# Relational graph layer on one core: x's high part by a rounding copy with a test of its low bits, VectorE's small steps with two inputs, and a new order in the head

## The chip, the cores and the metric

The kernel runs on one NeuronCore of a Trainium2 chip. The metric is the device time of one execution, in microseconds (us). A core has TensorE (PE) for matrix products, VectorE (DVE), ScalarE (ACT) and GpSimd (POOL) for elementwise work, and SyncE (SP), which here issues the large transfers. Each works through its own list in order and waits on semaphores for the others.

## What is computed

x is 8 x 1024 x 128 (fp32), adj is 8 x 1024 x 1024 (int32, here only 0 and 1), weight 4 x 128 x 128, bias 128. Per batch and relation the nodes' features are summed over the edges of that relation and projected, the input is added, and each row is normalised:

```python
masks = (relation[None] == rel_ids[:, None, None, None]).astype(x.dtype)
h = jnp.einsum('rbnm,bmd->rbnd', masks, x)
y = jnp.einsum('rbnd,rdo->bno', h, weight)
out = layernorm(x + y + bias)          # (v - mean) / sqrt(var + 1e-5) over the 128 features
```

With the inputs as drawn only relation 1 occurs. The kernel computes that case and counts on the way whether another value occurs; if one did, a general path behind a branch would be run (not entered here).

## The kernel before, in words

**Units and halves.** adj comes in 32 units of 1 MB (4 per batch, 256 target nodes each), x in 8 loads of 0.5 MB. Two units make a half (512 nodes), so there are 16 halves, called hf 0 to 15 below. SP issues the loads in the order unit 0, x of batch 0, unit 1, and so on; unit u waits until unit u - 8 has been masked (8 buffers), and x of batch b from batch 4 on until batch b - 4 has been added (4 buffers). The stores stand behind all loads in SP's list.

**Per unit.** VectorE turns the integers into bytes (`convert`, L429: min with 2, times 60, u32 to u8, 128 x 2048). TensorE transposes them as packed words (`turn`, L178). ScalarE expands the bytes into fp32r numbers (`expand`, L350).

**Per half.** TensorE multiplies the expanded mask by x in two parts, 8 matmuls of 512 columns each: `hi_products` with x_hi and `lo_products` with x_lo (L187). ScalarE copies the sum out of PSUM (`copy_half`, L357), TensorE spreads the bias (L194) and multiplies by the weights (L199, together `project_half`), VectorE adds x (`add_half`, L443) and takes statistics (L205, L210) and var + eps (`lift_variance`, L214), GpSimd raises that to the power -0.5 and makes the scale and shift of each row (`scales`: L307, L217, L312), and VectorE (`normalize`, L221) and ScalarE (L370) write two row groups each. The first and the last half go in quarters (256 nodes).

**The two parts of x, per batch.** VectorE masks x down to its upper 20 bits (`top`, L166, x_top), GpSimd copies x_top into x_hi as fp32r (`hi`, L297) and subtracts it from x (`lo`, L170, x_lo).

**The order.** All lists are written by hand. TensorE in the loop, for half hf: hi_products(hf), turn(2hf + 3), project_half(hf - 1), lo_products(hf), turn(2hf + 4). VectorE in the loop, for hf: convert(2hf + 4), convert(2hf + 5), on even hf top of the batch after the current one, add_half(hf - 1) with its statistics and var + eps, and normalize of half hf - 2. GpSimd: hi(b + 1), scales(2b - 1), lo(b + 1), scales(2b). In the head VectorE runs convert(0), top(0), `place_bias` (three copies of the bias's bf16 parts, L491), convert(1) to convert(3), top(1), convert(4) and on. Dummy matmuls (`keep_warm`, L605) fill TensorE's first waits.

## Time and profile before

| | before |
|---|---|
| runs | 119.49 us median of 3 (118.33 to 120.13) |
| the profiled execution | 118.53 us, span 116.7 us, mean granted TensorE clock 0.991 |
| busy | PE 102.6 us (88%), DVE 95.0 (81%), ACT 84.6 (72%), POOL 75.7 (65%) |
| loads and stores | 42.16 MB; HBM read 37.82 MB; mean 361 GB/s over the span |

The span is what the profile covers; the execution's own time lies 1.83 us above it. "Busy" leaves out waits, branches and the issuing of transfers. The whole-span shares mix a head (up to about 28 us), a steady stretch (28 to 104 us) and a tail. In the page's 40 slices the DMA engines are at nine tenths or more from the second slice to the 33rd, and TensorE from about the tenth.

### The profile page before, as it was taken

How to read it: one execution, taken by the hardware profiler on the slowest of the kernel's cores; microseconds unless marked ns; L12 is line 12 of the kernel's file. 1: busy time of each engine (PE TensorE's matmuls, PEld its weight loads, DVE VectorE, ACT ScalarE, POOL GpSimd, SP SyncE). 2: the span in 40 equal slices, each digit the busy share in tenths (PEclk: the TensorE clock that was granted, in tenths of full speed). 3: DMA queues.
4: the chain of work that ended last, by engine and by line, in shares of the span. 5: the costliest groups of instructions: out<-in, count | busy, mean ns of one | idle time of the engine just before them, and what ended most of it. 6: DMA issues, size and time to landing. Idle time of an engine off the chain costs nothing.

```text
span 116.7 us, 1943 instructions
## 1 busy us (share of the span) xinstructions
PE 102.6 (88%) x587; PEld 85.5 (73%) x587; DVE 95.0 (81%) x242; ACT 84.6 (72%) x114; POOL 75.7 (65%) x78
## 2 busy tenths in 40 slices
PE   5966379994999999999999999999999999999800
PEld 2333378683889888888898889898888888889600
DVE  0089967633989899999999999999999999996960
ACT  0433199179868997899999999999999889974410
POOL 6069038000095998599759898999899759953640
PEclk9999999999999999999999999999999999999996
DMA  3999999999999999999999999999999997030441
GB/s 87 396 433 429 415 438 427 415 432 418 418 424 424 424 424 417 417 424 424 414 431 421 414 428 413 429 413 427 421 427 418 404 420 314 10 142 38 171 152 53
DMA packets 7362, 42.16 MB, mean 361 GB/s; under 512 B 819, under 2 KB 1206, under 8 KB 3254
## 3 DMA queue, kind: packets, MB, share of 16 engines
q1 hardware_dynamic: 7200, 41.95, 86.9%
q8 instruction: 6, 0.10, 0.4%
q10 hardware_dynamic: 150, 0.07, 0.2%
q14 instruction: 6, 0.05, 0.1%
HBM read 37.82 MB, written 4.19 MB: 360 GB/s over the span
## 4 chain that ended last, share of the span: by engine, by line
PE 48%; DMA 21%; DVE 15%; POOL 8%; issue 3%; ACTq 1%; POOLq 0%; DVEq 0%
PE h_ps L187 32%; DMA adj_sb<-in_adj_dram 17%; PE y_ps L199 8%; PE tp_ps L178 7%; DMA bias_rows<-in_L_gnn_bias_dram 4%; DVE bias_parts L491 4%; POOL scale L217 4%; DVE mask L429 3%; DVE stats L205 3%; POOL x_lo L170 2%; DVE total L443 2%; PE y_ps L194 2%; DVE var_eps L214 2%; DVE mean_var L210 1%; ACTq L379 1%
## 5 line engine op out<-in xcount | busy, mean ns | idle before, releaser
L350 ACT ACTIVATE maskT<-tp_ps 128x2048 fp32r<-128x2048 fp8e5 x32 | 60.2, 1881 | 14.9 <-PE tp_ps L178 14.8
L429 DVE TENSOR_SCALAR mask<-adj_sb 128x2048 uint8<-128x2048 uint32 x32 | 39.5, 1267 | 12.4 <-DMA adj_sb<-in_adj_dram 12.4
L217 POOL TENSOR_TENSOR scale<-var_eps,power 128x4 f32<-128x4 f32 (+1 forms) x17 | 36.3, 2137 | 0.9 <-DVE var_eps L214 0.7
L187 PE MATMUL h_ps<-maskT,x_hi 128*128 128x512 f32 (+1 forms) x144 | 34.2, 379 | 2.6 <-ACT maskT L350 2.5
L187 PE MATMUL h_ps<-maskT,x_lo 128*128 128x512 f32 (+1 forms) x144 | 34.3, 380 | 0.4 <-POOL x_lo L170 0.4
L187 PEld LDWEIGHTS h_ps<-maskT,x_hi 128*128 128x128 f32 x144 | 24.3, 189 | 7.7 <-ACT maskT L350 3.9
L187 PEld LDWEIGHTS h_ps<-maskT,x_lo 128*128 128x128 f32 x144 | 24.1, 189 | 4.5 <-POOL x_lo L170 0.7
L178 PEld LDWEIGHTS tp_ps<-identity,mask 128*128 128x128 f32 x128 | 19.8, 202 | 6.4 <-DVE mask L429 2.7
L178 PE MATMUL tp_ps<-identity,mask 128*128 128x128 f32 x128 | 20.2, 281 | 3.4 <-DVE mask L429 3.4
L170 POOL TENSOR_TENSOR x_lo<-x_sb,x_top 128x1024 fp32r<-128x1024 f32 x8 | 19.2, 2402 | 0.0
L307 POOL TENSOR_SCALAR minus_mean<-mean_var 128x4 f32<-128x4 f32 (+1 forms) x16 | 4.0, 248 | 22.5 <-DVE var_eps L214 21.6
L199 PEld LDWEIGHTS y_ps<-w_sb,h_sb 128*128 128x128 f32 x128 | 16.7, 192 | 1.2 <-ACT h_sb L364 0.7
L199 PE MATMUL y_ps<-w_sb,h_sb 128*128 128x128 f32 x128 | 17.2, 276 | 0.3 <-ACT h_sb L364 0.3
L205 DVE BATCH_NORM_STATS2 stats<-total 128x6 f32<-128x128 f32 x64 | 14.1, 281 | 1.3
L370 ACT ACTIVATE out_sb<-total,shift,scale 128x128 f32<-128x128 f32 x31 | 13.5, 484 | 0.8 <-POOL shift L312 0.6
L297 POOL CAST x_hi<-x_top 128x1024 fp32r<-128x1024 f32 x8 | 8.3, 1041 | 6.9 <-DVE x_top L166 6.9
L357 ACT ACTIVATE h_sb<-h_ps 128x512 f32<-128x512 f32 x14 | 8.4, 599 | 5.5 <-issue 5.5
L443 DVE TENSOR_TENSOR total<-y_ps,x_sb 128x512 f32<-128x512 f32 (+1 forms) x17 | 11.0, 650 | 0.8 <-PE y_ps L199 0.8
L221 DVE TENSOR_SCALAR out_sb<-total,mean_var,scale 128x128 f32<-128x128 f32 x33 | 9.9, 339 | 0.6 <-POOL scale L217 0.6
L214 DVE TENSOR_SCALAR var_eps<-mean_var 128x4 f32<-128x4 f32 (+1 forms) x17 | 8.3, 485 | 1.7
L605 PE MATMUL h_ps<-warm 128*128 128x512 bf16 x24 | 7.6, 478 | 1.4 <-POOL warm L275 1.4
L312 POOL TENSOR_TENSOR shift<-minus_mean,scale 128x4 f32<-128x4 f32 (+1 forms) x16 | 6.0, 372 | 2.1
(30 smaller groups left out, 40.4 us busy)
## 6 DMA issues: line engine op xcount, KB each, us to landing
adj_sb<-in_adj_dram SPq DMA_DIRECT2D x32, 1024.0 KB, 18.0
x_sb<-in_x_dram SPq DMA_DIRECT2D x8, 512.0 KB, 12.1
out_dram<-out_sb SPq DMA_DIRECT2D x7, 512.0 KB, 18.5
out_dram<-out_sb SPq DMA_DIRECT2D x1, 256.0 KB, 2.3
out_dram<-out_sb SPq DMA_DIRECT2D x2, 128.0 KB, 2.6
w_sb<-in_L_gnn_weight_dram ACTq DMA_DIRECT2D x1, 64.0 KB, 7.1
bias_rows<-in_L_gnn_bias_dram ACTq DMA_DIRECT2D x3, 0.5 KB
```

The costliest lines, as they stand in the source:

```text
L170: eng.tensor_tensor(flat(x_lo[:, slot]), flat(x_sb[:, x_slot]), flat(x_top[:, :]).bitcast(fp32), ALU.subtract).then_inc(done, 1)
L178: last = nc.tensor.transpose(tp_ps[:, bank, place:place + P], words[:, o, j], identity[:, :])
L187: last = nc.tensor.matmul(h_ps[:, bank, 0:n], (x_hi, x_lo)[part][:, slot, t, :], maskT[:, places, t // WORD, t % WORD, :], start=(first an ...
L199: last = nc.tensor.matmul(y[:, n, :], h_of(r)[:, s], w_sb[:, r, :], start=False, stop=(r == relations - 1 and s == tiles.stop - 1))
L205: last = nc.vector.bn_stats(stats[:, slot, s, :], total[:, place, s, :])
L214: nc.vector.tensor_scalar(var_eps[:, slot, tiles], mean_var[:, slot, tiles, 1], EPS, None, ALU.add).then_inc(done, by)
L217: nc.gpsimd.tensor_tensor(scale[:, slot, tiles], var_eps[:, slot, tiles], power[:, tiles], ALU.pow).then_inc(done, by)
L221: last = nc.vector.tensor_scalar(out_sb[:, b, s, :], total[:, place, s, :], mean_var[:, slot, s, 0:1], scale[:, slot, s:s + 1], ALU.subtra ...
L350: nc.scalar.activation(maskT[:, u % NMT], turned_codes(u % NTP), ACT.Copy, accum_out=counts[:, u:u + 1]).then_inc(expanded, 1)
L370: last = nc.scalar.activation(out_sb[:, b, s, :], total[:, b % NTOTAL, s, :], ACT.Identity, bias=shift[:, b % 2, s:s + 1], scale=scale[:, ...
L429: nc.vector.tensor_scalar(mask[:, u % NMASK], adj_sb[:, u % NADJ].bitcast(u32), CAP, SET, ALU.min, ALU.mult).then_inc(masked, 1)
L443: nc.vector.tensor_tensor(total[:, b % NTOTAL, tiles], y, x_sb[:, b % NX, tiles], ALU.add).then_inc(added, by)
```

## The change

- **x's high part.** VectorE's mask of x and its buffer x_top go. x_hi is now a copy of x into fp32r, which rounds; x_lo is x minus x_hi. For batch 0 VectorE makes both itself, from batch 1 on GpSimd does.
- **The test.** Before its first var + eps (half 0) VectorE takes the low 12 bits of both slots of x_hi, finds their maximum and adds it to eps. If the copies left any low bit set, eps would become huge; otherwise it stays 1e-5.
- **Small steps.** `lift_variance` adds a tile eps in place of a constant; `normalize` takes the scale as a second tensor, broadcast over the row.
- **GpSimd's order.** lo follows hi at once, both ahead of the scales of the iteration, and lo(b) waits until unit 4b + 1 has been masked.
- **The head.** The bias copies are a quarter as wide and stand behind convert(2), since the matmul now broadcasts the bias itself. project_half(1) moves from behind turn(7) to behind turn(5), with ScalarE's copy_half(1) between expand(4) and expand(5).

VectorE's list from the add of half 0 to the next two masks, before (L429 is convert; the first row is convert(7), the rows after the stats belong to half 0, the last two rows are convert(8) and convert(9)):

```order
L429 TENSOR_SCALAR mask<-adj_sb 128x2048 [waits turned,adj_loaded7]
L443 TENSOR_TENSOR total<-y_ps,x_sb 128x512 [waits projected]
L205 BN_STATS stats<-total 128x6 [waits added]
L205 BN_STATS stats<-total 128x6 x3
L210 BN_AGGR mean_var<-stats 128x2 [waits measured]
L210 BN_AGGR mean_var<-stats 128x2 x3
L214 TENSOR_SCALAR var_eps<-mean_var 128x4 [waits aggregated]
L429 TENSOR_SCALAR mask<-adj_sb 128x2048 [waits turned,adj_loaded0]
L429 TENSOR_SCALAR mask<-adj_sb 128x2048 [waits turned,adj_loaded1]
```

The same place in the changed kernel (L433 is convert there, L450 the add):

```order
L433 TENSOR_SCALAR mask<-adj_sb 128x2048 [waits turned,adj_loaded7]
L450 TENSOR_TENSOR total<-y_ps,x_sb 128x512 [waits projected]
L204 BN_STATS stats<-total 128x6 [waits added]
L204 BN_STATS stats<-total 128x6 x3
L438 TENSOR_SCALAR low_bits<-x_hi 128x2048 [waits hi_made,const_set]
L441 TENSOR_REDUCE low_most<-low_bits 128x1 [waits low_found]
L443 TENSOR_TENSOR eps<-eps,low_most 128x8 [waits low_found]
L209 BN_AGGR mean_var<-stats 128x2 [waits measured,low_found]
L209 BN_AGGR mean_var<-stats 128x2 x3
L214 TENSOR_TENSOR var_eps<-mean_var,eps 128x4 [waits aggregated]
L433 TENSOR_SCALAR mask<-adj_sb 128x2048 [waits turned,adj_loaded0]
L433 TENSOR_SCALAR mask<-adj_sb 128x2048 [waits turned,adj_loaded1]
```

Three instructions, two of them over 2048 elements per partition, stand ahead of the masks of units 8 and 9.

GpSimd's list from the second scales on, before (x_hi and x_lo of batches 2 and 3; L307, L217 and L312 are one call of `scales`):

```order
L297 CAST x_hi<-x_top 128x1024 [waits multiplied,topped]
L307 TENSOR_SCALAR minus_mean<-mean_var 128x4 [waits var_ready]
L217 TENSOR_TENSOR scale<-var_eps,power 128x4
L312 TENSOR_TENSOR shift<-minus_mean,scale 128x4 [waits negated,scaled]
L170 TENSOR_TENSOR x_lo<-x_sb,x_top 128x1024
L307 TENSOR_SCALAR minus_mean<-mean_var 128x4 [waits var_ready]
L217 TENSOR_TENSOR scale<-var_eps,power 128x4
L312 TENSOR_TENSOR shift<-minus_mean,scale 128x4 [waits negated,scaled]
L297 CAST x_hi<-x_top 128x1024 [waits multiplied,topped]
```

And in the changed kernel:

```order
L300 CAST x_hi<-x_sb 128x1024 [waits multiplied,x_loaded2]
L168 TENSOR_TENSOR x_lo<-x_sb,x_hi 128x1024 [waits masked,hi_made]
L312 TENSOR_SCALAR minus_mean<-mean_var 128x4 [waits var_ready]
L217 TENSOR_TENSOR scale<-var_eps,power 128x4
L317 TENSOR_TENSOR shift<-minus_mean,scale 128x4 [waits negated,scaled]
L312 TENSOR_SCALAR minus_mean<-mean_var 128x4 [waits var_ready]
L217 TENSOR_TENSOR scale<-var_eps,power 128x4
L317 TENSOR_TENSOR shift<-minus_mean,scale 128x4 [waits negated,scaled]
L300 CAST x_hi<-x_sb 128x1024 [waits multiplied,x_loaded3]
```

The subtraction has moved from between the two scales to directly behind the copy.

The diff, without the tile and semaphore declarations, the general path and the renamed sites:

```diff
...
@@ -162,12 +164,8 @@
         def store(eng, b, place, tiles, done):
             eng.dma_start(out_p[b][:, tiles.start * D:tiles.stop * D], flat(out_sb[:, place, tiles])).then_inc(done, 16)
 
-        def take_top(x_slot, done):
-            nc.vector.tensor_scalar(flat(x_top[:, :]), flat(x_sb[:, x_slot]).bitcast(u32), TOP_BITS, None,
-                                    ALU.bitwise_and).then_inc(done, 1)
-
         def take_lo(eng, x_slot, slot, done):
-            eng.tensor_tensor(flat(x_lo[:, slot]), flat(x_sb[:, x_slot]), flat(x_top[:, :]).bitcast(fp32),
+            eng.tensor_tensor(flat(x_lo[:, slot]), flat(x_sb[:, x_slot]), flat(x_hi[:, slot]).bitcast(fp32),
                               ALU.subtract).then_inc(done, 1)
 
         def turn_words(of, bank, done):
@@ -191,7 +189,8 @@
 
         def spread_bias(y, tiles):
             n = tiles.stop - tiles.start
-            nc.tensor.matmul(y[:, 0:n, :], spread[:, :], bias_parts[:, 0:n, :], start=True, stop=False)
+            nc.tensor.matmul(y[:, 0:n, :], spread[:, :], bias_parts[:, :].unsqueeze(1).to_broadcast([P, n, D]),
+                             start=True, stop=False)
 
         def project(h_of, y, relations, tiles, done, by):
             for n, s in enumerate(range(tiles.start, tiles.stop)):
@@ -211,15 +210,16 @@
             last.then_inc(done, by)
 
         def lift_variance(slot, tiles, done, by):
-            nc.vector.tensor_scalar(var_eps[:, slot, tiles], mean_var[:, slot, tiles, 1], EPS, None, ALU.add).then_inc(done, by)
+            n = tiles.stop - tiles.start
+            nc.vector.tensor_tensor(var_eps[:, slot, tiles], mean_var[:, slot, tiles, 1], eps[:, 0:n], ALU.add).then_inc(done, by)
 
         def row_scales(slot, tiles, done, by):
             nc.gpsimd.tensor_tensor(scale[:, slot, tiles], var_eps[:, slot, tiles], power[:, tiles], ALU.pow).then_inc(done, by)
 
         def normalize(b, slot, place, tiles, done, by):
             for s in tiles:
-                last = nc.vector.tensor_scalar(out_sb[:, b, s, :], total[:, place, s, :], mean_var[:, slot, s, 0:1],
-                                               scale[:, slot, s:s + 1], ALU.subtract, ALU.mult)
+                last = nc.vector.scalar_tensor_tensor(out_sb[:, b, s, :], total[:, place, s, :], mean_var[:, slot, s, 0:1],
+                                                      scale[:, slot, s:s + 1].to_broadcast([P, D]), ALU.subtract, ALU.mult)
             last.then_inc(done, by)
 
         block = ctx.enter_context(nc.Block())
@@ -279,8 +279,9 @@
             nc.gpsimd.affine_select(identity[:, :], ones[:, :], [[-1, P]], ALU.is_equal, 0.0, base=0,
                                     channel_multiplier=1).then_inc(const_set, 1)
             nc.gpsimd.memset(power[:, :], -0.5).then_inc(const_set, 1)
+            nc.gpsimd.memset(eps[:, :], EPS).then_inc(const_set, 1)
             nc.gpsimd.memset(spread[:, :], 1.0).then_inc(const_set, 1)
-            nc.gpsimd.memset(bias_parts[:, :, :], 0.0).then_inc(bias_split, 1)
+            nc.gpsimd.memset(bias_parts[:, :], 0.0).then_inc(bias_split, 1)
 
             def split_bias():
                 pool.wait_ge(bias_loaded, 16 * len(PARTS))
@@ -291,12 +292,16 @@
                                         ALU.subtract).then_inc(bias_split, 1)
 
             def hi(b):
-                pool.wait_ge(topped, b + 1)
-                if b >= 2:
+                pool.wait_ge(x_loaded[b % NX], 16 * (b // NX + 1))
+                if b == 1:
+                    pool.wait_ge(lo_made, 1)
+                else:
                     pool.wait_ge(multiplied, CH * (b - 1))
-                nc.gpsimd.tensor_copy(flat(x_hi[:, b % 2]), flat(x_top[:, :]).bitcast(fp32)).then_inc(hi_made, 1)
+                nc.gpsimd.tensor_copy(flat(x_hi[:, b % 2]), flat(x_sb[:, b % NX])).then_inc(hi_made, 1)
 
             def lo(b):
+                pool.wait_ge(hi_made, b + 1)
+                pool.wait_ge(masked, CH * b + 2)
                 take_lo(nc.gpsimd, b % NX, b % 2, lo_made)
 
             def scales(b, tiles, count, by):
@@ -316,15 +321,12 @@
                 scales(hf // 2, HALF[hf % 2], 2 * (hf + 1), 2)
 
             split_bias()
-            hi(0)
-            lo(0)
             for b in range(B):
                 if b + 1 < B:
                     hi(b + 1)
+                    lo(b + 1)
                 if b >= 1:
                     scales_half(2 * b - 1)
-                if b + 1 < B:
-                    lo(b + 1)
                 scales_half(2 * b)
             scales(LAST, QUARTER[2], 2 * (HALVES - 1) + 1, 1)
             pool.wait_ge(var_ready, 2 * HALVES)
...
@@ -384,8 +385,11 @@
             expand(2)
             copy_quarter(0, 1)
             expand(3)
-            for hf in range(1, HALVES - 1):
-                if hf >= 2:
+            expand(4)
+            copy_half(1)
+            expand(5)
+            for hf in range(2, HALVES - 1):
+                if hf > 2:
                     copy_half(hf - 1)
                 expand(2 * hf + 2)
                 expand(2 * hf + 3)
@@ -429,12 +433,15 @@
                 nc.vector.tensor_scalar(mask[:, u % NMASK], adj_sb[:, u % NADJ].bitcast(u32), CAP, SET,
                                         ALU.min, ALU.mult).then_inc(masked, 1)
 
-            def top(b):
-                dve.wait_ge(x_loaded[b % NX], 16 * (b // NX + 1))
-                if b >= 1:
-                    dve.wait_ge(hi_made, b)
-                    dve.wait_ge(lo_made, b)
-                take_top(b % NX, topped)
+            def find_low_bits():
+                dve.wait_ge(hi_made, 2)
+                nc.vector.tensor_scalar(low_bits[:, :], x_hi[:, :].rearrange("p s t d -> p (s t d)").bitcast(u32), ~TOP_BITS & 0xFFFFFFFF, None,
+                                        ALU.bitwise_and).then_inc(low_found, 1)
+                dve.wait_ge(low_found, 1)
+                nc.vector.reduce_max(low_most[:, :], low_bits[:, :], AX.X).then_inc(low_found, 1)
+                dve.wait_ge(low_found, 2)
+                nc.vector.tensor_tensor(eps[:, :], eps[:, :], low_most[:, :].to_broadcast([P, TILES]), ALU.add).then_inc(low_found, 1)
+                dve.wait_ge(low_found, 3)
 
             def add(b, y, tiles, count, by):
                 dve.wait_ge(projected, count)
@@ -447,6 +454,10 @@
                 measure_rows(b % 2, b % NTOTAL, tiles, measured, by)
 
             def variances(b, tiles, count, by):
+                if count == 2:
+                    dve.wait_ge(const_set, 5)
+                if count == 2:
+                    find_low_bits()
                 dve.wait_ge(measured, count)
                 aggregate_rows(b % 2, tiles, aggregated, by)
                 dve.wait_ge(aggregated, count)
@@ -488,24 +499,24 @@
             def place_bias():
                 dve.wait_ge(bias_split, 3)
                 for q, part in zip(PARTS, (bias_rows, bias_rest, bias_fine)):
-                    last = nc.vector.tensor_copy(bias_parts[q:q + 1], upper(part[q:q + 1, :]).unsqueeze(1).to_broadcast(
-                        [1, HT, D]))
+                    last = nc.vector.tensor_copy(bias_parts[q:q + 1, :], upper(part[q:q + 1, :]))
                 last.then_inc(bias_split, 1)
 
             convert(0)
-            top(0)
+            dve.wait_ge(x_loaded[0], 16)
+            nc.vector.tensor_copy(flat(x_hi[:, 0]), flat(x_sb[:, 0])).then_inc(hi_made, 1)
+            dve.wait_ge(hi_made, 1)
+            take_lo(nc.vector, 0, 0, lo_made)
+            convert(1)
+            convert(2)
             place_bias()
-            for u in (1, 2, 3):
-                convert(u)
-            top(1)
+            convert(3)
             convert(4)
             convert(5)
             for hf in range(1, HALVES - 1):
                 for u in (2 * hf + 4, 2 * hf + 5):
                     if u < UNITS:
                         convert(u)
-                if hf % 2 == 0 and hf // 2 + 1 < B:
-                    top(hf // 2 + 1)
                 add_half(hf - 1)
                 measure_half(hf - 1)
                 if hf >= 2:
...
@@ -624,12 +635,14 @@
             turn(4)
             lo_products(1)
             turn(5)
+            project_half(1)
             turn(6)
             for hf in range(2, HALVES - 1):
                 hi_products(hf)
                 if 2 * hf + 3 < UNITS:
                     turn(2 * hf + 3)
-                project_half(hf - 1)
+                if hf > 2:
+                    project_half(hf - 1)
                 lo_products(hf)
                 if 2 * hf + 4 < UNITS:
                     turn(2 * hf + 4)
...
```

The declarations add `low_bits` (128 x 2048, u32), `low_most` (128 x 1) and `eps` (128 x 8), drop `x_top`, and make `bias_parts` 128 x 128.

## Rows read from the trace of the kernel before

**Rows 1.** The page: busy tenths, granted clock and GB/s moved in 40 slices of the span.
```profile
PE   5966379994999999999999999999999999999800
PEclk9999999999999999999999999999999999999996
GB/s 87 396 433 429 415 438 427 415 432 418 418 424 424 424 424 417 417 424 424 414 431 421 414 428 413 429 413 427 421 427 418 404 420 314 10 142 38 171 152 53
```

**Rows 2.** TensorE in order of time: start us, us, engine, line, what, [idle before <- releaser].
```profile
13.50 0.75 PE L178 MATMUL tp_ps<-identity,mask 128*128 128x128 f32 x4 [2.50 <-DVE mask L429]
...
33.43 0.63 PE L178 MATMUL tp_ps<-identity,mask 128*128 128x128 f32 x4
37.26 2.10 PE L187 MATMUL h_ps<-maskT,x_lo 128*128 128x512 f32 x8
39.20 0.63 PE L178 MATMUL tp_ps<-identity,mask 128*128 128x128 f32 x4
43.46 2.14 PE L187 MATMUL h_ps<-maskT,x_lo 128*128 128x512 f32 x8 [0.20 <-POOL x_lo L170]
...
101.68 2.13 PE L187 MATMUL h_ps<-maskT,x_lo 128*128 128x512 f32 x8 [0.17 <-POOL x_lo L170]
```

**Rows 3.** VectorE in order of time, from convert(7) to convert(8).
```profile
28.30 1.23 DVE L429 TENSOR_SCALAR mask<-adj_sb 128x2048 uint8<-128x2048 uint32 x1 [3.86 <-DMA adj_sb<-in_adj_dram]
29.44 0.68 DVE L443 TENSOR_TENSOR total<-y_ps,x_sb 128x512 f32<-128x512 f32 x1
30.16 0.87 DVE L205 BATCH_NORM_STATS2 stats<-total 128x6 f32<-128x128 f32 x4
31.07 0.38 DVE L210 BATCH_NORM_AGGREGATE mean_var<-stats 128x2 f32<-128x6 f32 x4
31.55 0.17 DVE L214 TENSOR_SCALAR var_eps<-mean_var 128x4 f32<-128x4 f32 x1
31.66 1.23 DVE L429 TENSOR_SCALAR mask<-adj_sb 128x2048 uint8<-128x2048 uint32 x1
```

**Rows 4.** Groups by line and form: count | busy us, mean ns | idle before them.
```profile
L443 DVE TENSOR_TENSOR total<-y_ps,x_sb 128x512 f32<-128x512 f32 x15 | 10.2, 681 | 0.8 <-PE y_ps L199 0.8
L443 DVE TENSOR_TENSOR total<-y_ps,x_sb 128x256 f32<-128x256 f32 x2 | 0.8, 414 | 0.0
```

**Rows 5.** VectorE in order of time, an undisturbed pass of the steady loop.
```profile
81.02 0.68 DVE L443 TENSOR_TENSOR total<-y_ps,x_sb 128x512 f32<-128x512 f32 x1
...
83.19 0.17 DVE L214 TENSOR_SCALAR var_eps<-mean_var 128x4 f32<-128x4 f32 x1
...
83.78 2.36 DVE L429 TENSOR_SCALAR mask<-adj_sb 128x2048 uint8<-128x2048 uint32 x2
86.05 0.68 DVE L443 TENSOR_TENSOR total<-y_ps,x_sb 128x512 f32<-128x512 f32 x1
```

**Rows 6.** GpSimd in order of time: a copy, two ends of scales, a subtraction.
```profile
46.88 1.05 POOL L297 CAST x_hi<-x_top 128x1024 fp32r<-128x1024 f32 x1 [0.61 <-DVE x_top L166]
51.98 0.20 POOL L312 TENSOR_TENSOR shift<-minus_mean,scale 128x4 f32<-128x4 f32 x1
...
75.15 0.20 POOL L312 TENSOR_TENSOR shift<-minus_mean,scale 128x4 f32<-128x4 f32 x1
75.30 2.39 POOL L170 TENSOR_TENSOR x_lo<-x_sb,x_top 128x1024 fp32r<-128x1024 f32 x1
```

**Rows 7.** VectorE in order of time, beside the scales and the subtraction.
```profile
49.43 2.38 DVE L429 TENSOR_SCALAR mask<-adj_sb 128x2048 uint8<-128x2048 uint32 x2
...
71.79 2.35 DVE L429 TENSOR_SCALAR mask<-adj_sb 128x2048 uint8<-128x2048 uint32 x2
76.25 1.47 DVE L214 TENSOR_SCALAR var_eps<-mean_var 128x4 f32<-128x4 f32 x1
```

**Rows 8.** The warm-up matmuls in order of time, the first two batches of them.
```profile
1.38 4.72 PE L605 MATMUL h_ps<-warm 128*128 128x512 bf16 x12 [1.38 <-POOL warm L275]
7.57 1.89 PE L605 MATMUL h_ps<-warm 128*128 128x512 bf16 x8
```

19 lines of the change are left out of this document (10 added, 9 removed).

## The prediction, made before the changed kernel was run

> **What bounds the kernel now.** I read the page first: TensorE's row of tenths stands at nine from the tenth slice on, with the granted clock at nine almost throughout, and the transfers move some 420 GB/s up to the 33rd [rows 1]. Then TensorE in order of time [rows 2]. From the start of the loop near 28 us it runs back to back: turn(8) starts at 33.43, turn(10) at 39.20, so one half takes **5.77 us**. From lo_products(3) at 37.26 to lo_products(14) at 101.68 there are 11 halves, 64.42 us, against 11 x 5.77 = 63.47: only 0.95 us is lost in all that time, and where the rows name a cause it is x_lo, late from GpSimd (43.46, 101.68). Whatever delays TensorE in this stretch delays the end by as much, since nothing behind it has slack to give back; whatever is saved there can be at most 0.95 us. The question is therefore when TensorE gets into its stride, and whether VectorE keeps ahead of it.
>
> VectorE's head [rows 3]: convert(1) to convert(3) stand behind the bias copies, and TensorE waits 2.50 us for the first of them [rows 2]. But convert(7) starts at 28.30 after 3.86 us of waiting for the transfer of unit 7. From there VectorE works in order: add at 29.44, statistics at 30.16, mean and variance at 31.07, var + eps at 31.55, convert(8) at 31.66.
>
> **The head.** Bias copies that are a quarter as wide and stand behind convert(2) let units 1 to 3 be masked as they arrive. VectorE takes on the copy and the subtraction of batch 0, about 0.7 us (1024 columns at a convert's pace) and 1.2 us (by the 1.04 ns per column worked out below), between convert(0) and convert(1), while unit 1 is still being loaded. With project_half(1) moved ahead, TensorE should be through hi_products(2) before unit 7 is masked. None of it moves the landing of unit 7, which was issued before anything that changes here. So convert(7) stays at 28.30 and is ready at 29.53; turn(7), project_half(1) being done already, and lo_products(2) (1.94 us to the next turn, 37.26 to 39.20 [rows 2]) let TensorE stand ready for turn(8) near 31.9 instead of 33.43. I book the head's repair at **0**: what it gains is waited away at the next point. The cover is the transfer of unit 7; were that earlier, the gain would show (see the rivals).
>
> **The test of low bits.** Three instructions stand on VectorE between the statistics of half 0 and convert(8). The masking of 128x2048 u32 has the input of a convert: 1.23 us [rows 3]. The maximum over 2048 columns has no row. The adds give (681 - 414) / 256 = 1.04 ns per column and 0.15 us fixed [rows 4], so 2048 columns make 2.28 us; the lower bound is a convert's 1.23, the upper the statistics' pace, 512 columns in 0.87 us, so 3.5 us [rows 3]. I take 2.28: one pass at the add's pace. The small add is 0.17, as var + eps, and three waits on its own results take 0.05 each. Sum 1.23 + 2.28 + 0.17 + 0.15 = 3.83 us, between 2.8 and 5.0. Then mean and variance start at 31.07 + 3.83 = 34.90, convert(8) 0.59 later at 35.49, its mask is ready at 36.72, and turn(8) starts near 36.78 instead of 33.43: **+3.35 us**, between +2.3 and +4.6. It is not hidden: TensorE's list is in order, turn(8) stands ahead of hi_products(3), and TensorE waits for it some 4.9 us.
>
> **x's parts, without x_top.** Eight masks of x leave VectorE, and x_lo is made an iteration and more before lo_products wants it. The 0.95 us of the steady stretch goes: **-0.95**. VectorE's pass without a mask of x is 86.05 - 81.02 = 5.03 us [rows 5], well under 5.77.
>
> But GpSimd now holds VectorE at another place. The trace shows that the two exclude each other: var + eps, normally 0.17 us, took 1.47 at 76.25, until the x_lo of 75.30 + 2.39 had ended, and VectorE's next converts with it [rows 6, 7]. In the changed list the scales of the odd pass are followed by hi and lo in one go. Two calls show when the scales end: their last step started 0.17 us after the end of the two converts beside it in one (51.98 against 49.43 + 2.38), 1.01 us after in the other (75.15 against 71.79 + 2.35) [rows 6, 7]. The copy starts 0.15 us after that and takes 1.05, the subtraction 0.05 later 2.39: it ends 3.81 to 4.65 us after the converts. The next convert would start 5.03 - 2.36 = 2.67 us after them [rows 5] and is held 1.14 to 1.98 us.
>
> The first such place is convert(10). With convert(8) at 35.49 the pair ends at 37.85, the subtraction of batch 2 at 41.66 to 42.50, and mask 10 is ready at 42.9 to 43.7; TensorE wants it at 36.78 + 5.77 = 42.55. That costs 0.35 to 1.2 us, **+0.8**. Later, two passes take 10.06 + (1.14 to 1.98) = 11.2 to 12.0 us against TensorE's 11.54: 0 to 0.5 us in each of five pairs. The middle is 0.1 over: **+0.4**, between 0 and 2.5.
>
> **Small steps and tail.** var + eps and normalize change their form. var + eps and two normalizes took 0.59 us of a pass (83.19 to 83.78) [rows 5]; two normalizes at 128 x 1.04 ns + 0.15 us alone would be 0.57. Booked at 0, since they stand where VectorE is ahead; what they could cost at most is the first rival below. The narrower bias copies and the broadcast bias matmul: 0; they stand in waits of the head.
>
> **Sum.** +3.35 - 0.95 + 0.8 + 0.4 = +3.6 us. On the profiled execution's 118.53 that makes 122.1; that execution is 0.96 under the median of the runs, from which it would be 123.1. I forecast **122.6 us**, between the two. With the bounds (+2.3 - 0.95 + 0.35 to +4.6 - 0.95 + 1.2 + 2.5) this case covers 120.2 to 126.8, and I hold 121.0 to 124.9 for its likely part.
>
> **Rivals.**
>
> *VectorE becomes the bound, because the new small steps are held too.* The rows leave open whether a step with two inputs from SBUF waits for GpSimd: the only such form before is the add, whose first input is PSUM, and its 15 instances average 0.681 us, hence never waited long [rows 4]. If they wait, the var + eps and two normalizes, 0.59 us by the rows of a pass, come behind the subtraction rather than ahead of it: a pair takes 11.8 to 12.6, 0.3 to 1.1 us over TensorE's, 0.7 x 5 = 3.5 in place of 0.4, and the first place costs 0.6 more. Together +3.7: about 126. It decides once a pair exceeds 11.54 us. For it speaks that both inputs must be read at once; against it that VectorE then gains what it waits less elsewhere. The Trainium skill, "SBUF — State Buffer", section "Who interferes with whom", says that a VectorE instruction with two SBUF inputs contends with a GpSimd instruction that reads SBUF, which speaks for this rival and against what the change does to the small steps; no row here shows such an instruction. Chance 0.15.
>
> *TensorE's clock falls in the 4.9 us wait for turn(8).* The granted clock of the trace stays at full until the tail [rows 1]; its longest wait is 2.50 us, and the 13.50 row behind it is quick [rows 2]. But the first 12 warm-up matmuls took 4.72 us, 393 ns each, the later eight 236 ns [rows 8]: after idleness it ran at the pace of its lower level for about 4 us and lost some 2. If that comes again: about 124.6. The Trainium skill, "TensorE: Matmul & The Clock Gate", section "What's actually happening", has the clock halved after idleness; this trace has no wait long enough to tell. Chance 0.15.
>
> *Not slower: unit 7 lands earlier.* Its wait of 3.86 us is long against the 2.5 us that a megabyte takes at the page's some 420 GB/s [rows 1, 3]. Were it masked 2.3 us earlier, at 26.0, turn(8) would start at 34.4, +1.0 us; with -0.95 and the collisions at their lower bound of 0.35 the sum is +0.4, 119 to 120. From 3.35 us earlier on the test costs nothing. For it speaks that units before it came evenly; against it that the order of issue up to unit 8 is the same. Halfway, at 26.9, it gives 121 to 121.5. Chance 0.25, a fifth of it faster by over 2%, where VectorE's freed time also does more than I can see.
>
> **Chances and range.** 2% of 119.49 is 2.4 us, about what a measurement of this kernel can tell from no change. The forecast case has 0.45, of which a tenth of all chances lies below 121.9. Slower by over 2%: 0.35 + 0.15 + 0.15 = 0.65, and with a little of the last rival 0.67. Within 2%: 0.28. Faster: 0.05. The range that should hold 8 in 10 is 120.2 to 126.0.
>
> **What would show it.** In the new profile: a wait of TensorE of 4 to 5 us for mask 8 between about 32 and 37 us; a reduce of low_bits near 2.3 us; convert(8) near 35.5; then 5.77 us per half with no wait for x_lo; single waits for masks where the subtraction stands beside a convert that took up to 3 us; matmuls of 8 in 2.1 us right after the long wait, if the clock held. I am wrong if convert(8) starts before 33, if unit 7's mask is well before 28.3, or if TensorE keeps losing time for masks through the whole loop.

## The result, and the profile after

The changed kernel takes **122.99 us** (median of 4 runs, 122.8 to 123.46) against 119.81 us for the kernel before beside it (4 runs, 118.33 to 120.8): a ratio of **1.035** [1.025, 1.045], slower. Its profiled execution took 122.80 us, span 121.1, mean granted clock 0.977. Ratios, here and below, compare of either kernel only the runs within 1.5% of its fastest, so they differ somewhat from the ratios of the medians. The time lies 0.4 us from the 122.6 forecast; the sum behind it is right in its main term and wrong in two others, which nearly cancelled.

The page of the kernel after, as in [rows 1]: busy tenths, granted clock and GB/s in 40 slices.

```profile
PE   5988799976609999999999999999999999999800
PEclk9999999999995899999999999999999999999996
GB/s 89 403 430 429 424 424 425 411 425 428 420 425 422 425 406 430 425 417 421 429 414 422 421 429 420 409 430 425 420 422 413 402 260 0 0 41 133 156 158 54
```

TensorE has a hole in slices 11 and 12 (6, 0), and right behind it the granted clock falls for two slices (5, 8). Neither is in the rows of before.

VectorE in order of time, answering to [rows 3]:

```profile
28.29 1.23 DVE L433 TENSOR_SCALAR mask<-adj_sb 128x2048 uint8<-128x2048 uint32 x1 [2.34 <-DMA adj_sb<-in_adj_dram]
...
30.94 1.21 DVE L438 TENSOR_SCALAR low_bits<-x_hi 128x2048 uint32<-128x2048 uint32 x1
32.19 2.29 DVE L441 TENSOR_REDUCE low_most<-low_bits 128x1 f32<-128x2048 uint32 x1
34.51 0.17 DVE L443 TENSOR_TENSOR eps<-eps,low_most 128x8 f32<-128x8 f32 x1
...
35.30 2.36 DVE L433 TENSOR_SCALAR mask<-adj_sb 128x2048 uint8<-128x2048 uint32 x2
...
39.79 2.72 DVE L221 SCALAR_TENSOR_TENSOR out_sb<-total,mean_var,scale 128x128 f32<-128x128 f32 x2
42.43 2.35 DVE L433 TENSOR_SCALAR mask<-adj_sb 128x2048 uint8<-128x2048 uint32 x2
```

convert(7) still starts when unit 7 lands. Behind it stand the mask of the low bits, the reduce of 2.29 us and the small add; convert(8) starts at 35.30, 3.64 us later than before. Further down two normalizes took 2.72 us, held by the x_lo that GpSimd was making (it ended at 42.36); convert(10) waited for them, and mask 10 was ready at 43.6, within the 42.9 to 43.7 of the prediction.

TensorE in order of time, answering to [rows 2]:

```profile
36.58 1.00 PE L176 MATMUL tp_ps<-identity,mask 128*128 128x128 f32 x4 [4.38 <-DVE mask L433]
37.23 3.52 PE L185 MATMUL h_ps<-maskT,x_hi 128*128 128x512 f32 x8
40.58 0.63 PE L176 MATMUL tp_ps<-identity,mask 128*128 128x128 f32 x4
...
44.04 0.63 PE L176 MATMUL tp_ps<-identity,mask 128*128 128x128 f32 x4
...
105.87 2.12 PE L185 MATMUL h_ps<-maskT,x_lo 128*128 128x512 f32 x8
```

turn(8) starts 3.15 us later than before, after a wait of 4.38 us. Eight matmuls behind it take 3.52 us instead of some 2.1, and turn(9) starts 4.00 us after turn(8). Before it was 2.34 (33.43 to 35.77): 1.66 us lost to the clock. TensorE then runs without a wait for x_lo to lo_products(14), 4.19 us later than at 101.68. The windows of the same stretch say what the clock was. Each row has the stretch, its length, the busy time of PE, PEld, DVE, ACT and POOL (with the number of instructions), the granted clock, the DMA share and GB/s:

```profile
32.00:36.50 4.50, 0.20 (x1) 0.00 (x0) 4.29 (x10) 0.89 (x3) 0.97 (x1) 1.00 1.02 424
36.50:38.00 1.50, 1.42 (x6) 1.32 (x7) 1.50 (x3) 0.39 (x1) 1.50 (x2) 0.64 0.99 415
38.00:40.60 2.60, 2.60 (x9) 2.00 (x8) 2.43 (x12) 1.58 (x2) 2.39 (x4) 0.55 1.01 422
40.60:46.00 5.40, 5.40 (x33) 4.72 (x32) 5.37 (x7) 4.45 (x6) 4.42 (x4) 1.00 1.01 417
```

0.55 to 0.64 of full speed while TensorE was busy again: mostly the lower level, 1.2 GHz. At 40.6 it was back at 2.4. Through the wait itself it still stood at full; it fell as TensorE resumed.

Two rows of the steady loop show GpSimd beside VectorE, answering to [rows 6, 7]; first GpSimd (scale, shift, x_hi, x_lo), then VectorE:

```profile
47.28 1.39 POOL L217 TENSOR_TENSOR scale<-var_eps,power 128x4 f32<-128x4 f32 x1
48.80 1.02 POOL L317 TENSOR_TENSOR shift<-minus_mean,scale 128x4 f32<-128x4 f32 x1
49.76 1.03 POOL L300 CAST x_hi<-x_sb 128x1024 fp32r<-128x1024 f32 x1
50.87 2.39 POOL L168 TENSOR_TENSOR x_lo<-x_sb,x_hi 128x1024 fp32r<-128x1024 f32 x1
```

```profile
46.88 0.60 DVE L221 SCALAR_TENSOR_TENSOR out_sb<-total,mean_var,scale 128x128 f32<-128x128 f32 x2
47.41 2.35 DVE L433 TENSOR_SCALAR mask<-adj_sb 128x2048 uint8<-128x2048 uint32 x2
...
51.79 1.49 DVE L214 TENSOR_TENSOR var_eps<-mean_var,eps 128x4 f32<-128x4 f32 x1
...
53.73 2.35 DVE L433 TENSOR_SCALAR mask<-adj_sb 128x2048 uint8<-128x2048 uint32 x2
```

var + eps in its two-input form is held, 1.49 us instead of 0.16, until x_lo ends at 53.26. But the power at 47.28 takes only 1.39 us, beside the converts. In the kernel before it mostly ended behind the converts and averaged 2.32 us; three of its instances beside a pair of converts were short there too, this one among them:

```profile
54.87 1.38 POOL L217 TENSOR_TENSOR scale<-var_eps,power 128x4 f32<-128x4 f32 x1
```

In the changed kernel all ten that start during a normalize with converts behind it take 1.39 or 1.40 us. The pair of converts that starts at 53.73 has its like two passes later at 65.10, so two passes take 11.37 us, under TensorE's 11.60: the loop loses nothing.

### The profile page after: what moved, and what is told of

Read it like the earlier page. It is cut to its first block, busy times and chain, and to the rows that moved or that the text cites. A ratio compares the mean times of both kernels' runs of the same rounds, so it can differ in the third digit from the quotient of the medians.

```text
span 121.1 us, 1941 instructions
## 1 busy us (share of the span) xinstructions
PE 105.0 (87%) x586; PEld 86.4 (71%) x587; DVE 93.8 (77%) x239; ACT 84.8 (70%) x114; POOL 64.3 (53%) x77
## 3 DMA queue, kind: packets, MB, share of 16 engines
HBM read 37.82 MB, written 4.19 MB: 347 GB/s over the span
## 4 chain that ended last, share of the span: by engine, by line
PE 61%; DMA 18%; DVE 9%; SPq 4%; issue 3%; POOL 1%; POOLq 0%; DVEq 0%
PE h_ps L185 39%; DMA adj_sb<-in_adj_dram 18%; PE tp_ps L176 10%; PE y_ps L198 10%; SPq L159 3%; PE y_ps L192 2%; DVE low_most L441 2%; DVE stats L204 2%; DVE total L450 1%; SPq L162 1%; DVE mask L433 1%; DVE low_bits L438 1%; POOL scale L217 1%; DVE mean_var L209 1%; DVE out_sb L221 1%
## 5 line engine op out<-in xcount | busy, mean ns | idle before, releaser
L433 DVE TENSOR_SCALAR mask<-adj_sb 128x2048 uint8<-128x2048 uint32 x32 | 38.0, 1219 | 16.2 <-DMA adj_sb<-in_adj_dram 16.2
L185 PE MATMUL h_ps<-maskT,x_hi 128*128 128x512 f32 (+1 forms) x144 | 35.8, 392 | 0.4 <-ACT maskT L351 0.3
L185 PEld LDWEIGHTS h_ps<-maskT,x_hi 128*128 128x128 f32 x144 | 25.4, 198 | 5.7 <-ACT maskT L351 1.4
L176 PE MATMUL tp_ps<-identity,mask 128*128 128x128 f32 x128 | 21.1, 288 | 7.6 <-DVE mask L433 7.6
L217 POOL TENSOR_TENSOR scale<-var_eps,power 128x4 f32<-128x4 f32 (+1 forms) x17 | 23.1, 1358 | 0.7 <-DVE var_eps L214 0.7
L312 POOL TENSOR_SCALAR minus_mean<-mean_var 128x4 f32<-128x4 f32 (+1 forms) x16 | 4.0, 251 | 31.3 <-DVE var_eps L214 31.3
L168 POOL TENSOR_TENSOR x_lo<-x_sb,x_hi 128x1024 fp32r<-128x1024 f32 x7 | 16.8, 2394 | 5.8 <-DVE mask L433 5.3
L450 DVE TENSOR_TENSOR total<-y_ps,x_sb 128x512 f32<-128x512 f32 (+1 forms) x17 | 11.0, 649 | 2.6 <-issue 1.8
L221 DVE SCALAR_TENSOR_TENSOR out_sb<-total,mean_var,scale 128x128 f32<-128x128 f32 x33 | 12.2, 408 | 0.6 <-POOL scale L217 0.6
L317 POOL TENSOR_TENSOR shift<-minus_mean,scale 128x4 f32<-128x4 f32 (+1 forms) x16 | 11.0, 689 | 2.4 <-POOL scale L217 0.5
L300 POOL CAST x_hi<-x_sb 128x1024 fp32r<-128x1024 f32 x7 | 7.2, 1035 | 6.3 <-DMA x_sb<-in_x_dram 6.3
L214 DVE TENSOR_TENSOR var_eps<-mean_var,eps 128x4 f32<-128x4 f32 (+1 forms) x17 | 9.2, 540 | 1.6
```

Of the source, the lines that this page charges most:

```text
L168: eng.tensor_tensor(flat(x_lo[:, slot]), flat(x_sb[:, x_slot]), flat(x_hi[:, slot]).bitcast(fp32), ALU.subtract).then_inc(done, 1)
L176: last = nc.tensor.transpose(tp_ps[:, bank, place:place + P], words[:, o, j], identity[:, :])
L185: last = nc.tensor.matmul(h_ps[:, bank, 0:n], (x_hi, x_lo)[part][:, slot, t, :], maskT[:, places, t // WORD, t % WORD, :], start=(first an ...
L217: nc.gpsimd.tensor_tensor(scale[:, slot, tiles], var_eps[:, slot, tiles], power[:, tiles], ALU.pow).then_inc(done, by)
L221: last = nc.vector.scalar_tensor_tensor(out_sb[:, b, s, :], total[:, place, s, :], mean_var[:, slot, s, 0:1], scale[:, slot, s:s + 1].to_b ...
L317: nc.gpsimd.tensor_tensor(shift[:, b % 2, tiles], minus_mean[:, b % 2, tiles], scale[:, b % 2, tiles], ALU.mult).then_inc(shifted, by)
```

## The experiments

The eleven kernels came in several sets, each with its own runs of the kernel before. Those runs spread from 117.2 to 121.6 us, so differences well under 1 us between sets rest on the traces, not on the medians.

### 1. Without the test

```diff
-                if count == 2:
-                    find_low_bits()
```

> The changed kernel without the three instructions of the low-bits test (low_bits, low_most and the add to eps); the check on x_hi is left out, the rest is computed. Theory A (the test delays TensorE at turn(8), and the long wait brings its clock down): convert(8) at about 31.7 us, or when its unit lands, turn(8) near 32.9 instead of 36.6, no slow matmuls behind it, the granted clock of the span back near 0.99; x_lo never late; span about 121.1 - 3.7 - 1.7 = 115.7 to 116.2, time about 117.8, 1 to 1.5% under the kernel before. Rival B (the delay comes from GpSimd's new order and the two-input steps): at most 1 us less than the changed kernel, about 122.

Measured 118.8 us (118.32 to 119.14), ratio 1.002 [0.998, 1.006]. So **the test costs 4.2 us** of the changed kernel's time (122.99 against 118.8), all of the change's loss. The kernel comes out 1 us above the 117.8 expected, and TensorE in order of time says where:

```profile
33.10 0.75 PE L176 MATMUL tp_ps<-identity,mask 128*128 128x128 f32 x4 [0.81 <-DVE mask L433]
...
40.13 0.74 PE L176 MATMUL tp_ps<-identity,mask 128*128 128x128 f32 x4 [0.95 <-DVE mask L433]
```

turn(10) waits 0.95 us, since var + eps is held there by batch 2's x_lo. VectorE of the same kernel:

```profile
36.61 1.81 DVE L214 TENSOR_TENSOR var_eps<-mean_var,eps 128x4 f32<-128x4 f32 x1
```

That is the collision at mask 10 of the prediction (+0.8). In the full change nothing shows of it, since TensorE, slowed by its clock, came later than the mask.

### 2. The test in the head's waits

```diff
+            take_low_bits()                # behind convert(5)
...
+                    if u == 6:
+                        find_low_most()    # reduce and add, ahead of convert(7)
...
-                    find_low_bits()
+                    dve.wait_ge(low_found, 3)
```

> The changed kernel with the same test cut in two and moved into VectorE's two waits for transfers in the head: the masking of the low bits behind convert(5), the maximum and the add to eps behind convert(6). Theory A: the waits of 2.7 and 2.3 us (before convert(6) and convert(7)) hold 1.2 and 2.5 us of work, so convert(7) is at most 0.3 us late, the x_lo of batch 1 starts about 1 us later without being late for lo_products(2), and the time is that of the kernel without the test within 0.4 us, about 118: the test costs nothing, only its place did. Rival B (the head is too tight: the masking and x_lo exclude each other and hold convert(6) and turn(6)): convert(7) or turn(6) slips by 1 us or more and the time is 119 to 120.

Measured 119.23 us (119.04 to 119.56), 1.007 [1.001, 1.012]: 0.4 us over no test, 3.8 under the change. VectorE:

```profile
21.95 1.22 DVE L438 TENSOR_SCALAR low_bits<-x_hi 128x2048 uint32<-128x2048 uint32 x1
24.62 1.85 DVE L433 TENSOR_SCALAR mask<-adj_sb 128x2048 uint8<-128x2048 uint32 x1 [1.45 <-DMA adj_sb<-in_adj_dram]
26.39 2.27 DVE L443 TENSOR_REDUCE low_most<-low_bits 128x1 f32<-128x2048 uint32 x1
28.78 1.23 DVE L433 TENSOR_SCALAR mask<-adj_sb 128x2048 uint8<-128x2048 uint32 x1
```

The reduce, 2.27 us again, lies in the wait for unit 7; convert(7) is 0.4 late, because convert(6) took 1.85 beside batch 1's x_lo. The test's place is its cost.

### 3. TensorE kept busy in the wait

```diff
                 lo_products(hf)
+                if hf == 2:
+                    for _ in range(18):
+                        nc.tensor.matmul(h_ps[:, 0, :], warm[:, 0:P], warm[:, :], start=True, stop=True)
```

> The changed kernel with 18 dummy matmuls of 512 columns between lo_products(2) and turn(8), about 3.9 us of work in the 4.4 us that TensorE waits there; their product is thrown away. Theory A (1.66 us of the loss is the clock's, turn(8) to turn(9) in 4.00 us against 2.34): turn(8) stays at 36.6, turn(9) follows in 2.34 us, the granted clock returns to about 0.99, span 1.5 to 1.7 us shorter, about 121.3 us. It could be up to 1 us less, since VectorE's mask 10 (ready at 43.7) is then wanted at 42.4. Rival B (the slow matmuls behind the wait have another cause, such as the transfers or the weights): turn(9) still takes 4.0 us, time as the changed kernel or longer.

Measured 122.36 us (122.23 to 122.46), 1.035 [1.032, 1.039]. TensorE:

```profile
31.87 4.06 PE L649 MATMUL h_ps<-warm 128*128 128x512 bf16 x18
36.43 0.75 PE L176 MATMUL tp_ps<-identity,mask 128*128 128x128 f32 x4 [0.49 <-DVE mask L433]
36.93 2.12 PE L185 MATMUL h_ps<-maskT,x_hi 128*128 128x512 f32 x8
38.88 0.63 PE L176 MATMUL tp_ps<-identity,mask 128*128 128x128 f32 x4
...
43.56 0.75 PE L176 MATMUL tp_ps<-identity,mask 128*128 128x128 f32 x4 [1.06 <-DVE mask L433]
```

The clock held: 2.12 us for the eight matmuls, turn(9) 2.45 after turn(8). But of 1.55 us saved only 0.6 reach the end (0.5 by the spans), because now turn(10) waits 1.06 us. The clock's loss and the collision at mask 10 lie over each other; alone the first costs 1.6 us and the second 1.0.

### 4. The test alone, on the kernel before

The test and the tile eps (set by GpSimd, read by var + eps as a scalar), and nothing else of the change; the call:

```diff
             def variances(b, tiles, count, by):
+                if count == 2:
+                    dve.wait_ge(const_set, 5)
+                    find_low_bits()
```

> The kernel before with the test alone, at the same place as in the change (eps as a tile that var + eps reads as a per-row scalar). Theory A (the test is nearly the whole of the loss): convert(8) near 35.4, turn(8) near 36.6, TensorE's wait is 3.1 us here since its head is not repaired; if the clock falls as in the changed kernel +4.8 us, if not +3.2 us, against the kernel before: 122.7 to 124.3 us. Rival B (the test costs no more than VectorE's idle time): under 1 us more, about 120.3.

Measured 122.26 us (121.55 to 123.63), 1.034 [1.024, 1.045], as much as the whole change, but by another way than expected. Unit 7 had landed at 26.91, so convert(8) started at 33.95 and mask 8 was ready at about 35.2; turn(8) started at 35.51 without a wait. In this execution the test delayed no turn. TensorE was 2.08 us late there (33.43 before) through the head:

```profile
14.46 1.13 PE L182 MATMUL tp_ps<-identity,mask 128*128 128x128 f32 x4 [3.20 <-DVE mask L434]
15.24 2.06 PE L191 MATMUL h_ps<-maskT,x_lo 128*128 128x256 f32 x8
...
93.62 2.12 PE L191 MATMUL h_ps<-maskT,x_lo 128*128 128x512 f32 x8 [0.28 <-POOL x_lo L174]
```

Here the 3.20 us wait for mask 1 was enough for the clock to fall: 2.06 us for eight matmuls of 256 columns that take 1.20 in the kernel before, granted clock 0.50 from 14 to 17 us. (The bias's rows arrived later: GpSimd began to split them at 8.07 us, in the kernel before at 6.79, and the bias copies stand ahead of mask 1.) The loop lost 1.9 us more: from lo_products(3) to lo_products(14) it took 66.33 us against 64.42, with six waits for x_lo like the last row, and the power took 3.33 to 3.94 us each of the ten times that it started just ahead of converts. Whether the test brought that about isn't shown. So this kernel doesn't give the test's price; experiments 1 and 2 do. Unit 7's landing, on which my third rival stood, differs by 1.6 us between executions (26.91 to 28.47 over the eleven profiled ones in which the mask waits for it alone).

### 5. The head's repair alone

The edits of `spread_bias`, `place_bias`, project_half(1) and the order of the head, as in the diff of the change; x's parts, small steps and GpSimd's order as before.

> The kernel before with the head's repair alone: narrow bias copies behind convert(2), the bias broadcast by the matmul, project_half(1) and copy_half(1) ahead; x_top, GpSimd's order and the one-input steps as before, no test. Theory C (the head's worth is that TensorE's clock no longer falls in its wait for mask 1; where it held, as in the profiled execution of before, it is worth nothing): mask 1 ready at 12.6 instead of 13.5, held by GpSimd's first x_lo; granted clock of the span 0.985 or more in every run, time 118 to 118.7 with a spread under 1 us, against 117.8 to 121.1 for the kernel before. Rival D (the spread of the kernel before has another cause): spread over 2 us here too. If a half still takes 5.77 us here, the 5.80 of the changed kernel comes from neither the bias's broadcast nor the head.

Measured 118.3 us (12 runs, 117.12 to 120.47) against 119.51 (24 runs), 0.995 [0.990, 1.001]. The wait for mask 1 shrinks from 2.50 to 1.76 us and turn(8) starts at 32.63, 0.8 earlier, with convert(7) at 27.99. Near 0, as booked, and if anything a gain.

Theory C failed in its signs: the runs spread over 3.35 us and not under 1, at granted clocks of 0.971 to 0.994, as rival D had it. The profiled execution is one of the longer ones (119.27 us), though its clock never fell before the tail. What it lost lies in the loop, 65.89 us from lo_products(3) to lo_products(14) against 64.42, mostly where x_lo came late:

```profile
102.46 2.13 PE L187 MATMUL h_ps<-maskT,x_lo 128*128 128x512 f32 x8 [0.17 <-POOL x_lo L170]
```

So the spread of the kernel before has at least one cause beside the clock.

### 6. The small steps with one input

```diff
-            nc.vector.tensor_tensor(var_eps[...], mean_var[...], eps[:, 0:n], ALU.add)
+            nc.vector.tensor_scalar(var_eps[...], mean_var[...], eps[:, 0:1], None, ALU.add)
...
-                last = nc.vector.scalar_tensor_tensor(..., scale[:, slot, s:s + 1].to_broadcast([P, D]), ...)
+                last = nc.vector.tensor_scalar(..., scale[:, slot, s:s + 1], ...)
```

> The changed kernel with var + eps and normalize in their one-input form (eps and the scale as per-row scalars). Theory E (both forms are held by GpSimd's copy and subtraction until these end, so the form changes nothing): var + eps takes up to 1.5 us beside x_lo, the first normalize pair up to 2.7, turn(8) at 36.6 and the clock's fall as in the changed kernel, time 122.5 to 123.3. Rival F (the two-input form is what is held, or what spares GpSimd's power of 1.4 us against 2.1): the DVE rows beside x_lo are short, or the power takes 2 us and more again, and TensorE waits for masks in the loop, 0.5 us or more either way.

Measured **126.12 us** (125.48 to 126.47), 1.065 [1.060, 1.070]: 3.1 us slower than the change, where my theory said no difference. GpSimd and then VectorE, both with one-input steps:

```profile
47.55 3.33 POOL L217 TENSOR_TENSOR scale<-var_eps,power 128x4 f32<-128x4 f32 x1
...
51.16 1.04 POOL L300 CAST x_hi<-x_sb 128x1024 fp32r<-128x1024 f32 x1
52.27 2.49 POOL L168 TENSOR_TENSOR x_lo<-x_sb,x_hi 128x1024 fp32r<-128x1024 f32 x1
...
67.00 1.40 POOL L217 TENSOR_TENSOR scale<-var_eps,power 128x4 f32<-128x4 f32 x1
```

```profile
47.15 0.60 DVE L221 TENSOR_SCALAR out_sb<-total,mean_var,scale 128x128 f32<-128x128 f32 x2
47.66 2.36 DVE L433 TENSOR_SCALAR mask<-adj_sb 128x2048 uint8<-128x2048 uint32 x2
...
52.19 2.66 DVE L221 TENSOR_SCALAR out_sb<-total,mean_var,scale 128x128 f32<-128x128 f32 x2
54.77 1.24 DVE L433 TENSOR_SCALAR mask<-adj_sb 128x2048 uint8<-128x2048 uint32 x1
```

The power starts 0.1 us ahead of the convert as in the change, but ends 0.9 us behind both converts (3.33 us). The scales, x_hi and x_lo all end later, and the converts wait longer: from 54.77 to 67.14, two passes take 12.37 us, over TensorE's 11.6. TensorE then waits for a mask in each pair, five times between 56 and 106 us, four of them 0.46 to 0.48. The power is not long every time: four of the nine that start during a normalize with converts behind it take 1.39 or 1.40 us, as at 67.00. Each of these follows directly on an x_lo that had held the normalizes.

### 7. Which of the two small steps

The change with one of the two steps back in the one-input form: first var + eps, then the normalizes.

> The changed kernel with var + eps in its one-input form again (scalar eps[:, 0:1]) and the normalizes left with two inputs. Theory G: what the two-input form is worth (122.99 against 126.12 us) comes from the normalizes. GpSimd's power starts 0.1 us before the first convert in both kernels (47.28 against 47.41, and 47.55 against 47.66), so it isn't its own start that differs but what VectorE executes just then: a two-input normalize leaves it a way in, a one-input one doesn't. Then this kernel takes 123.0 us (122.6 to 123.4), power 1.4 us each time, two passes 11.4 us. Theory V: var + eps does it, since it stands directly ahead of GpSimd's three steps. Then 126.1 us, power 3.3 us beside free converts. Both in part: 124 to 125.5.

> The changed kernel with the normalizes in their one-input form and var + eps left with two inputs. Theory G: 126.1 us (125.7 to 126.5), power 3.3 us beside free converts, two passes near 12.4 us or, with var + eps held by x_lo instead of the normalizes, the same. Theory V: 123.0 us, power 1.4.

Measured 123.02 us (122.68 to 123.41) with the normalizes in two-input form, 125.73 (125.47 to 125.77) with var + eps in it. The power at the same place, of the first kernel and of the second:

```profile
47.51 1.38 POOL L217 TENSOR_TENSOR scale<-var_eps,power 128x4 f32<-128x4 f32 x1
```

```profile
47.39 3.34 POOL L217 TENSOR_TENSOR scale<-var_eps,power 128x4 f32<-128x4 f32 x1
```

All but 0.4 us of the 3.1 is **the normalizes' form**. Over the thirteen profiled executions, count the powers on 128x4 that start during a normalize with converts behind it: with two-input normalizes all 72 took 1.38 to 1.40 us, with one-input ones 14 of 58 took 1.37 to 1.40 and the other 44 took 2.51 to 3.95. So a two-input normalize always let the power in, and a one-input one mostly made it wait for the converts too; what lets in the 14 isn't shown. var + eps is held by x_lo in either form (1.50 us at 52.02 in the first kernel, with one input).

### 8. x_lo of batch 2 earlier

On top of experiment 2, GpSimd makes x_hi and x_lo of batch 2 ahead of the first scales.

```diff
+                if b == 2:
+                    pool.wait_ge(low_found, 1)     # in hi
...
-                pool.wait_ge(masked, CH * b + 2)
+                if b != 2:
+                    pool.wait_ge(masked, CH * b + 2)
...
+                if b == 0:
+                    hi(2)
+                    lo(2)
```

> The version with the test in the head's waits (masking behind convert(5), maximum behind convert(6)), and besides the x_hi and x_lo of batch 2 made on GpSimd ahead of the first scales, when it otherwise idles from 25 to 32 us. Theory G (the 1.05 us that TensorE waits for mask 10 there comes from x_lo of batch 2 holding var + eps and normalize): turn(10) follows turn(8) in 5.8 us instead of 7.1, no wait, span 1.0 us shorter: 118.2 us, 1.3% under the median of the kernel before's runs. Rival H (the copy and the subtraction then hold convert(6), convert(7) or the masking in the head): turn(7) or turn(8) slips by as much, 119.2 as without the move.

Measured 119.23 us (118.73 to 119.58), 1.009 [1.006, 1.012]: nothing gained on experiment 2. turn(10) no longer waits, but the subtraction (27.47 to 29.85) now holds the small add ahead of convert(7):

```profile
28.72 1.15 DVE L452 TENSOR_TENSOR eps<-eps,low_most 128x8 f32<-128x8 f32 x1
```

convert(7) starts at 29.80, 1.0 us later than in experiment 2. The collision was moved, as rival H had it.

### 9. The kernel before with TensorE kept busy in the head

```diff
             hi_quarter(0, 0)
+            keep_warm(10)
             turn(1)
```

> The kernel before with 10 dummy matmuls of 512 columns ahead of turn(1), 2.1 us of work in TensorE's 2.5 us wait for mask 1; their product is thrown away. Theory C: the clock no longer falls in the head, granted clock of the span 0.985 or more in every run, 118 to 118.6 us with a spread under 1 us. Rival D: spread and clock as in the kernel before, 117.8 to 121.1 us at 0.957 to 0.993.

Measured 118.01 us (median of 12 runs; eleven of them 117.04 to 119.14) against 119.51 (24 runs, 117.17 to 121.58), 0.997 [0.992, 1.001]. The ten matmuls take 2.33 us and leave a wait of 0.82:

```profile
10.99 2.33 PE L605 MATMUL h_ps<-warm 128*128 128x512 bf16 x10
14.14 0.74 PE L178 MATMUL tp_ps<-identity,mask 128*128 128x128 f32 x4 [0.82 <-DVE mask L429]
```

The eleven runs had a granted clock of 0.983 to 0.995; the runs of the kernel before went from 0.954 to 0.995, and all 14 above 119 us had 0.954 to 0.98. That fits a clock that falls in some executions of the kernel before in its wait for mask 1. But five of its ten other runs, 117.9 to 118.6 us, had 0.971 to 0.974 all the same, and with the clock kept up the eleven runs still spread over 2.1 us, not under 1 as theory C had it. Nor is the gain of the profiled execution (117.52 us) over that of the kernel before (118.53) the clock's, which was at full up to the tail in both: turn(8) starts 0.6 us later here, and the loop takes 63.32 us from lo_products(3) to lo_products(14) against 64.42, with no wait for x_lo. It is the fastest version found, 1.5 us under the kernel before in the median, and not distinguishable from it by 2%.

### 10. Both gains on the kernel before

Experiment 9 with the normalizes in two-input form.

> The kernel before with ten dummy matmuls ahead of turn(1) and the normalizes in two-input form: the two edits that seemed to help, without the test and without the new order of GpSimd. Theory G: power takes 1.4 us instead of a mean of 2.1, x_lo is made up to 1 us earlier, TensorE's waits for x_lo in the loop (0.95 us) go, and VectorE has room (5.77 us per half against 5.6 with a mask of x). 117.2 us (116.8 to 117.6), against 118.0 for the dummies alone. Theory V: no change from the dummies alone, 118.0 us (117.6 to 118.4). A rival: x_lo, started earlier, now stands beside the two-input normalizes and holds them, a mask comes late, and it is 118.5 or more.

Measured 118.87 us (118.47 to 119.3), no better than 118.01. The rival came true. Beside the converts the power took 1.38 or 1.39 us, but for one that started within a convert (2.29), and x_lo came early enough that TensorE never waited for it; but x_lo (39.02 to 41.42) then stood beside convert(11):

```profile
39.21 3.29 DVE L429 TENSOR_SCALAR mask<-adj_sb 128x2048 uint8<-128x2048 uint32 x1 [0.51 <-DMA adj_sb<-in_adj_dram]
```

3.29 us instead of 1.23. From turn(10) to turn(12) TensorE took 6.94 us (39.46 to 46.40) instead of 5.77, which is more than x_lo's waits had cost.

## Why the prediction was right, and where not

- **Head, 0.** Right: 0.995 [0.990, 1.001] with the head alone, and turn(8) at 33.10 without the test against 33.43 before.
- **Test, +3.35.** Right in place and size: low_bits 1.21, reduce 2.29 (2.28 taken), turn(8) at 36.58 (36.78), a wait of 4.38 (4.9). The overlap of the mask with the last statistics was missing from the sum. With what the wait brought with it, the test costs 4.2.
- **Rival, the clock falls in the wait.** It got 0.15 and came true: 1.66 us (it would have added 2). The step that failed was reading a clock at full behind a wait of 2.50 us as evidence for one behind 4.9 [rows 1, 2]. The Trainium skill, "TensorE: Matmul & The Clock Gate", section "What's actually happening", has the clock halved after idleness; here it fell after 4.38 us in the change, after 3.20 in experiment 4, and not in the profiled executions of experiments 3 and 9, whose waits were filled.
- **Collision at convert(10), +0.8.** The mechanism was right, 0.95 to 1.06 us in experiments 1 and 3. It gave 0 in the change, since the clock's loss covered it. In experiment 3 both stand in the same stretch, and they don't add.
- **Later collisions, +0.4.** Wrong: 0. The working took the scales to end up to 1.01 us after the converts; they end with them (49.82 against 49.76), because the power takes 1.4 us.
- **Small steps, 0; rival, VectorE becomes the bound.** Wrong, and the largest mistake. As the change has them they are worth 2.7 to 3.1 us: with one-input steps two passes take 12.37 us, more than the 12.0 I gave as the upper end, and the kernel 126.12. I had read the row of power (what it waits for) without asking what VectorE executes as it starts. The rival was right that two-input steps are held, but one-input ones are held as long (var + eps 1.50 us, two normalizes 2.66), so what it named is no cost of the form, and it had the wrong sign for the sum. The Trainium skill, "SBUF — State Buffer", section "Who interferes with whom", says that a VectorE instruction with two SBUF inputs contends with a GpSimd instruction that reads SBUF. The trace agrees (var + eps 1.49 us beside x_lo), but by that rule alone the form is a cost, and measured the normalizes' two-input form is a gain. The same section also says that a `tensor_scalar` can enter a mode in which it takes the port pair shared with GpSimd, that whoever issues first has the pair for the whole instruction, and that the other is then blocked entirely. The 44 long powers of the count in experiment 7 fit that, if the one-input normalize and the converts behind it (also `TENSOR_SCALAR`) are in that mode; the 14 short ones it doesn't explain, and the section doesn't name the two-input normalize's form (`SCALAR_TENSOR_TENSOR`). I had weighed the first rule and not the second.
- **x's parts, -0.95.** Right: no wait for x_lo after 40 us. A half takes 5.80 instead of 5.77 us, +0.33 over 11 halves; its cause is open. It is 5.76 to 5.77 with the head's repair alone and with the dummies alone, and 5.80 also without the test and, where no mask is awaited, with one-input steps; that leaves x's parts and GpSimd's order.
- **Rival, unit 7 lands earlier.** It didn't in the change (28.29 against 28.30), but in the profiled executions of experiments 4 and 9 it did (26.91, 27.01), with nothing in their edits that concerns the loads.

Together, at lo_products(14): +3.15 + 1.66 - 0.95 + 0.33 = +4.19 us, the 105.87 against 101.68 of the trace. By the trace the tail adds 0.2, and the spans differ by 4.4. The prediction's +3.6 came to the right time with +1.2 booked for collisions that didn't count and nothing for the clock's 1.66. The cause was forecast rightly; that the time came within 0.4 us was luck. One reading was off by a slice: TensorE's tenths in [rows 1] stand at nine from the eleventh, not the tenth; nothing rests on it.

## What to carry to other kernels

A one-off check costs what it delays, not what it takes: 0.4 us in the head's waits, 4.2 behind the first statistics. A wait of some microseconds on TensorE is priced with the clock behind it (here 1.66 us behind 4.38), and where two losses fall into the same stretch, the later one counts only for what the first leaves. Where VectorE and GpSimd share SBUF, look at which form of instruction is running on VectorE when a short GpSimd step starts: in this kernel it took 1.4 us in all 72 cases that began beside a two-input normalize, and 2.5 to 3.95 in 44 of the 58 that began beside a one-input one.

## What the runs showed of the hardware that was not expected

- The power on 128x4 took 1.38 to 1.40 us in all 72 cases in which it started during a two-input normalize of VectorE with converts behind it, and 2.51 to 3.95 us in 44 of 58 with a one-input one (the other 14: 1.37 to 1.40). The two forms themselves are equally long, 0.60 us for two normalizes. The runs show that the form matters (experiments 6 and 7); by which port or mode, and what else has a say with the one-input form, they don't show.
- TensorE's clock fell after a wait of 3.20 us in the head in one profiled execution and stayed at full after 2.50 us in another; eight matmuls of 256 columns took 2.06 against 1.20 us.
- A reduce over 2048 u32 took 2.29 us, the pace of a two-input add; a mask of the same size 1.21.
- One of the 12 runs of experiment 9 took 155.18 us at a granted clock of 0.662. No other run was like it, and no trace shows its cause.
